# A six-layer Perceiver block on one core: experts' scores asked for one tile further ahead, unit rows on GpSimd, context loads in the scores' loop, two bias products moved forward

## The reference, cut to what matters

```python
x = x + L0_xattn(layernorm(x), ctx_1024, ...)
x = x + L0_attn(layernorm(x), ...)            # state space
x = x + L0_ffn(layernorm(x), ...)             # soft mixture of 16 experts, 16 slots each
x = x + L1_xattn(layernorm(x), ctx_1024, mask, ...)
x = x + L1_attn(layernorm(x), ...)            # causal attention
x = x + L1_ffn(layernorm(x), ...)             # routed linear, 8 experts

def L0_ffn(x, ln_gamma, ln_beta, mu, scale, w1, b1, w2, b2):
    xn = layernorm(x, ln_gamma, ln_beta)
    x_unit, mu_unit = l2norm(xn, axis=-1), l2norm(mu, axis=0)
    logits = einsum('bnd,des->bnes', x_unit * scale, mu_unit)
    dispatch = softmax(logits, axis=1)                       # over the 32 tokens of a batch
    combine = softmax(logits.reshape(B, N, E * S), axis=-1)  # over the 256 slots
    slot_in = einsum('bnd,bnes->besd', xn, dispatch)
    h = gelu(einsum('besd,edh->besh', slot_in, w1) + b1)
    slot_out = einsum('besh,ehd->besd', h, w2) + b2
    return einsum('besd,bnes->bnd', slot_out, combine)

def L1_ffn(x, tile_sigs, W, b):
    idx = argmax(einsum('bsd,td->bst', x, sign(tile_sigs)), axis=-1)
    return (einsum('bsd,tde->bste', x, W) + b)[.., idx, :]
```

## Time and profile before

| | us |
|---|---|
| median of three runs | 985.24 |
| the three runs | 984.61, 985.24, 1930.26 |
| the profiled execution | 986.62 |
| its span, first to last instruction | 984.8 |

### The profile page before, as it was taken

The page is one execution under the profiler, slowest core; times in us unless marked ns, Lnnn a source line. Parts: engine busy times, 40 slices in busy tenths (PEclk is TensorE's granted clock), DMA queues, the critical chain, the costliest instruction groups (busy, mean ns, idle before and its releaser), DMA issues. The chain is left out here.

```text
span 984.8 us, 25493 instructions
## 1 busy us (share of the span) xinstructions
PE 815.8 (83%) x9286; PEld 448.7 (46%) x9286; DVE 726.6 (74%) x2428; ACT 563.4 (57%) x1419; POOL 201.6 (20%) x216
## 2 busy tenths in 40 slices
PE   5899999998867687887764577789698799999887
PEld 2577777776323233333231255456466334343343
DVE  5688888886389999989999588256565376767856
ACT  3798889889666658458415167445243533333345
POOL 1376676666000000000000012000310000000036
PEclk9999999999978789789867799799699899999989
DMA  8111111100000000000000250400183000000001
GB/s 251 34 40 46 37 43 37 38 21 2 1 0 0 1 0 1 1 1 1 0 1 1 82 99 1 173 4 4 44 322 150 1 1 1 1 1 1 1 13 32
DMA packets 23422, 36.67 MB, mean 37 GB/s; under 512 B 5668, under 2 KB 19748, under 8 KB 21156
## 3 DMA queue, kind: packets, MB, share of 16 engines
q1 hardware_dynamic: 23336, 35.53, 11.7%
HBM read 34.48 MB, written 1.05 MB: 36 GB/s over the span
## 5 line engine op out<-in xcount | busy, mean ns | idle before, releaser
L496 ACT ACTIVATE xa_prob<-xa_s,xa_nmax 128x257 f32<-128x257 f32 x256 | 128.1, 503 | 21.0 <-DVE xa_nmax L633 19.3
L780 POOL TENSOR_TENSOR xa_prob<-xa_prob,xa_rinv 128x1028 f32<-128x1028 f32 x64 | 121.6, 1902 | 76.8 <-DVE xa_rinv L640 75.9
L633 DVE CUSTOM_DVE_ANT_0 xa_s<-xa_s_ps,xa_nbias 128x257 f32<-128x257 f32 x256 | 93.1, 420 | 12.4 <-ACT xa_prob L496 6.4
L1764 POOL TENSOR_TENSOR mo_disp_t<-mo_disp_t,mo_rst 128x256 f32<-128x256 f32 x16 | 9.9, 617 | 362.8 <-DVE mo_rst L1734 362.8
L326 PE MATMUL xa_t_ps<-identity,xa_prob 128*128 128x128 f32 x512 | 69.5, 279 | 3.6 <-ACT xa_p_t L505 1.8
L623 DVE COPY xa_kvs<-xa_kv_ps 128x512 f32<-128x512 f32 x64 | 44.1, 689 | 34.4 <-PE xa_kv_ps L300 34.4
L2523 ACT COPY ca_z<-ca_z_ps 128x512 f32<-128x512 f32 x64 | 37.5, 586 | 50.7 <-PE ca_z_ps L2399 50.7
L326 PEld LDWEIGHTS xa_t_ps<-identity,xa_prob 128*128 128x128 f32 x512 | 54.8, 141 | 25.2 <-issue 25.2
L2399 PE MATMUL ca_z_ps<-ca_xn_t,ca_m_t 128*128 128x512 f32 x128 | 64.2, 631 | 0.7 <-ACT ca_xn_t L2516 0.7
L505 ACT COPY xa_p_t<-xa_t_ps 128x1024 f32<-128x1024 f32 x64 | 63.5, 992 | 1.8 <-PE xa_t_ps L326 1.8
L939 PE MATMUL ss_bank<-ss_xs,ss_wx 128*128 128x512 f32 x128 | 60.2, 620 | 5.0 <-DVE ss_eps L1393 3.1
(11 more groups left out here) (369 smaller groups left out, 1898.6 us busy)
## 6 DMA issues: line engine op xcount, KB each, us to landing
xa_ctx_t<-in_ctx_t SPq DMA_DIRECT2D x64, 128.5 KB, 2.1
room<-in_ctx_t SPq DMA_DIRECT2D x8, 1028.0 KB, 6.5
room<-in_ctx_n SPq DMA_DIRECT2D x8, 1024.0 KB, 4.7
ss_wx<-in_ss_wx SPq DMA_DIRECT2D x1, 2048.0 KB, 7.7
xres<-in_x SPq DMA_DIRECT2D x4, 256.0 KB, 5.3
out_x<-xres SPq DMA_DIRECT2D x4, 256.0 KB, 2.3
ma_mask_u<-in_mask SPq DMA_DIRECT2D x4, 128.5 KB
room<-in_ca_wk SPq DMA_DIRECT2D x1, 512.0 KB, 3.5
```

The source lines that it names most:

```text
L496: nc.scalar.activation(prob[:, r, g, :], s_sb[:, b, g, :], ACT.Exp, bias=nmax[:, r, g:g + 1], scale=-1.0, accum_out=rsum[:, r, g:g + 1]).t ...
L633: nc.vector.tensor_tensor_reduce(out=s_sb[:, b, g, :], in0=s_ps[:, g, 0:S], in1=nbias[:, g, :], scale=1.0, scalar=3e38, op0=ALU.add, op1=A ...
L780: nc.gpsimd.tensor_tensor(prob[:, r, :, :], prob[:, r, :, :], bc(rinv[:, r, :].rearrange("p (g o) -> p g o", o=1), (P, G, S)), ALU.mult).t ...
```

## The change

Four edits, none of which adds or takes away arithmetic.

1. Scores one tile further ahead. PE transposes the unit rows of tile t+3 (not t+2) in turn t and computes the scores of tile t+2 ahead of the transposes of tile t's results. Three tiles are transposed before the loop instead of two. ACT copies tile t+3's transposed rows, takes the exponentials of tile t+1, and only then the squares (turn 5) or the roots (now turn 6).
2. Twelve of the thirteen unit rows of ACT go to POOL (one multiplication per tile, in the turn before its own), the other to DVE, ahead of the loop. On DVE what rides along (centring, scaling, the two tiny steps) now stands between `maxima` and `scales` of a turn instead of behind them. The scores' two PSUM buffers are banks 0 and 2 of `mo_lj_ps`, not 0 and 1, and the joins use neighbouring banks.
3. The four context loads are issued by SP in the first block, as soon as the eighth join's products are done, not in the second block.
4. In the routed layer the bias products of tiles 0 and 1 come ahead of the experts' products of the same tile.

```diff
-            return lj_ps[:, n % 2:3:2 - n % 2, SLOTS:2 * SLOTS].rearrange("p s (i c) -> p s i c", i=2)
+            return lj_ps[:, n % 2:n % 2 + 2, SLOTS:2 * SLOTS].rearrange("p s (i c) -> p s i c", i=2)
...
-        l_ps = lj_ps[:, 0:2, :]
+        l_ps = lj_ps[:, 0:3:2, :]
...
+        @block.sync
+        def _(sp):
+            sp.wait_ge(join_mm, JOINS)
+            for keys_first in (False, True):
+                for u in range(2):
+                    load_context(sp, d, ctx, u, u, keys_first)
...
-                    last = nc.tensor.matmul(lj_ps[:, 2 if h % 2 else n % 2, SLOTS + h // 2 * D:SLOTS + h // 2 * D + D],
+                    last = nc.tensor.matmul(lj_ps[:, n % 2 + h % 2, SLOTS + h // 2 * D:SLOTS + h // 2 * D + D],
...
-            for t in range(2):
-                turn_x(t, t)
-                logits(t, t)
+            turn_x(0, 0)
+            turn_x(1, 1)
+            logits(0, 0)
+            turn_x(2, 0)
+            logits(1, 1)
 
             for t in range(T):
-                if t + 2 < T:
-                    turn_x(t + 2, t % 2)
-                turn(t, t % 2)
+                if t + 3 < T:
+                    turn_x(t + 3, 1 - t % 2)
                 if t + 2 < T:
                     logits(t + 2, t % 2)
+                turn(t, t % 2)
                 if FIRST <= t < FIRST + JOINS:
                     join(t - FIRST)
...
             xut(0, 0)
             xut(1, 1)
+            xut(2, 0)
             exps(0, 0)
 
             for t in range(T):
+                if t + 3 < T:
+                    xut(t + 3, 1 - t % 2)
+                if t + 1 < T:
+                    exps(t + 1, 1 - t % 2)
                 if t == 5:
                     last_squares()
-                if t == 7:
+                if t == 6:
                     last_roots()
-                if t + 2 < T:
-                    xut(t + 2, t % 2)
-                if t + 1 < T:
-                    exps(t + 1, 1 - t % 2)
-                if t + 3 < T:
-                    unit(t + 3, 1 - t % 2)
                 out(t, t % 2)
...
             unit(2, 0)
+            unit(3, 1)
             maxima(0, 0)
             scales(0, 0)
 
             for t in range(T):
                 if t + 1 < T:
                     maxima(t + 1, 1 - t % 2)
-                if t + 1 < T:
-                    scales(t + 1, 1 - t % 2)
-                if FIRST <= t < FIRST + JOINS and t % 2 == 1:
-                    joined_values(t - FIRST)
                 if t < 2:
                     centred(AHEAD + 2 * t)
                     centred(AHEAD + 2 * t + 1)
...
                 if t == 7:
                     last_units()
+                if t + 1 < T:
+                    scales(t + 1, 1 - t % 2)
+                if FIRST <= t < FIRST + JOINS and t % 2 == 1:
+                    joined_values(t - FIRST)
 
         @block.gpsimd
         def _(pool):
+            def unit(t, j):
+                pool.wait_ge(xut_mm, t - 1)
+                if t == AHEAD:
+                    pool.wait_ge(unit_ready, 1)
+                nc.gpsimd.tensor_scalar(xu[:, j, :], x1[:, t, :], sums[:, t:t + 1], None, ALU.mult).then_inc(xu_ready, 1)
+
             for t in range(T):
+                if 0 < t and t + 3 < T:
+                    unit(t + 3, 1 - t % 2)
                 pool.wait_ge(rst_ready, t + 1)
...
             for t in range(T):
+                if t < 2:
+                    own_bias(t)
                 experts(t)
-                own_bias(t)
+                if t >= 2:
+                    own_bias(t)
```

19 lines of the change are left out of this document (4 added, 15 removed).

## The result

The changed kernel takes 975.94 us (median of 4 runs, 974.84 to 976.36) against 985.11 us of the kernel before: a ratio of 0.989 over all runs, with a 95% interval from 0.9872 to 0.9908. By the medians that is 9.2 us less, twice the 4.5 us of the forecast. It lies between the two prices of the rival in which PE's gaps in the second block go with the loads (977.0 us for half of them, 973.4 us for all), and by the 2% bound it counts as no change.

A forecast was written before the change was run, and what follows sets the result against it. DVE was taken to bound the scores' block and PE the second block. Savings of 2.16 + 1.76 - 0.25 + 0.86 = 4.53 us from 985.24 gave 980.7 us (chance 0.66), with a range from 975.0 to 984.6 us.

The forecast's parts named there:

- PE's gaps in the second block go with the loads: Rival, second block: PE's 7.3 us of gaps vanish with the context loads, 973.4 us, half of it 977.0; chance 0.14.
- Context loads: Scores' block: SP issues the loads some 11 us sooner, nothing waits for them either way; counted as nothing.
- Riders between maxima and scales: Scores' tiles 1 to 4 on DVE: 3.63 to 3.09 us each, four save 2.16 us (0.88 at the other end).
- Squares behind the exponentials: Scores' tile 6: 3.45 us in place of 5.21, 1.76 us saved, of which 0.6 might be lost.
- Unit rows on POOL: Scores' loop: ACT loses 13 multiplications, POOL gains 12; no gain or loss for unit rows from 0.29 up to 2 us.
- Scores one tile ahead: Scores' block: gains nothing by itself, costs 0.25 us once at the start, between 0.1 and 0.4.
- Library reload: POOL reloads its library in front of the first unit row; counted as nothing, after a gap of 0.27 us before.
- POOL starts late: Rival, scores' loop: a reload of two turns (5.58 us) gives back 3.2 us of the gain, 983.9 us; chance 0.08.
- Bias products first: Routed layer: DVE starts on tile 2 sooner, PE's wait of 0.86 us goes; 0.86 us saved, between 0.2 and 1.0.
- Slower: the gaps spread: Rival, second block: the nine calm tiles get PE's gaps too, 11.0 us more, 991.7 us; chance 0.05.
- the change doesn't do what it says: Rival: riders hide nothing, squares still hold DVE, only the bias products help, 984.4 us; chance 0.07.

## Why the prediction was right and wrong, point by point

- *Context loads*: the step that failed. The prediction put the move of the loads at nothing; the second block gave 8.0 us (7.6 us in the profile of the kernel with this edit alone, 8.3 us by its median). "I count nothing" left out that a fetch of PE's program that comes late beside the loads sets PE back for several tiles. The rival had it at 7.3 us and a chance of 0.14. Both of its observations against were true, and neither was against it: the gaps go on with a DMA share of 0.02 because the lag outlives the loads, and they fall at fixed distances because PE's program is fetched in pieces of fixed length. I took "it comes at fixed places" for "it is not caused by something in time". A fetch that is late once stays late in each piece until a place in the list that gives it back, and both signs follow from that.
- *Riders between maxima and scales*: right in kind, 2.9 us in place of 2.16. A tile became 2.90 and not 3.09 us. I added two durations of 0.30 us, but in a row of such instructions the next starts before the one ahead of it has ended by its row: from 567.72 to 568.31 us two that show 0.67 us together push the reciprocal back by 0.59, and in later tiles by 0.52. The pair also hid in 0.30 us of wait plus the end of the subtraction.
- *Squares behind the exponentials*: 1.90 us for tile 6, forecast 1.76. But it isn't theirs alone. With the slack of the other two edits the squares cost 0.58 us ahead of the exponentials. The gain of 1.9 is what the moves give together.
- *Unit rows on POOL*: counted 0, worth 0.71 us in the loop, since ACT's lateness had cost 0.15 us at each join and 0.3 at tile 8. The length was 0.61 and not 0.3 us. "Up to 2 us alike" fell: at 1.8 us the loop lost 1.77 us, through DVE's instructions and not through a wait.
- *Scores one tile ahead*: 0.27 us at the start as forecast (0.25). Together with the unit rows it was not without gain.
- *Library reload*: right, a gap of 0.07 us. *POOL starts late* did not come.
- *Bias products first*: 0.94 us in the layer, forecast 0.86, but that is luck. The layer before had 6.0 us of low clock and after 2.9 us; against the kernel with the loads alone and 3.0 us of it the gain is 39.43 - 39.30 = 0.13 us. PE's wait did not go; it grew from 0.86 to 1.47 us, because PE was done sooner and DVE's reading moved with it. And 1.7 us were lost between the second block and the layer. The edit has no visible part in that: the changed kernel with the bias products put back took 251.50 us there, near the 251.83 of after, and the same code took from 250.15 to 255.02 us over all profiles of this study. By the whole time the edit is not measurable.
- *Slower: the gaps spread* did not come; nor did *the change doesn't do what it says*.
- Without the loads' term the sum was close: 4.9 to 5.3 us measured for the rest, 4.5 forecast. That is in part luck. The loop, the start and the layer gave 5.29 - 0.27 + 0.94 = 5.96 us by the stages, 1.4 more than forecast, and stages that the change leaves alone lost 3.3 us in this execution. The range held the time, since it reached into the rival.

## What to carry to other kernels

Where PE runs hundreds of short products in a few microseconds, read its unexplained gaps together with the packets of its instruction queue, and keep bulk loads away from the moment of a fetch. The price is not paid during the load alone but, in the first half of the block here, in every piece behind it. Issue such loads beside a stage whose engines run few and long instructions, as the scores here, whose tiles stayed at 2.79 us with 4 MB in flight. And before a wait of PE is counted as time to be won, compare the granted clock with and without it.

## What the runs showed of the hardware that I had not expected

- A fetch of PE's program (by the reading of the packets above) that fell into 1 to 4 MB of loads some microseconds old came late, by some 2 to 3.5 us, and PE stood still until 0.9 to 1.6 us behind its end. Where it did so in the first half of the block, the pieces behind it had gaps of 0.3 to 1.6 us, up to the eighth piece, and the fifteen tiles lost 4.1 to 8.0 us; in the second half they lost 3.7 us and no lag stayed. Three kernels (squares back, unit rows on ACT, three multiplications on POOL) had two or three such gaps, 0.9 to 2.0 us in all, with no load in the block at all, and the same packets late by some 140 to 155 instructions; their fifteen tiles took 58.57, 58.88 and 56.82 us. A fourth (riders back) had one of 0.48 us. The largest of these gaps:

```profile
637.47 0.98 PE L1849 MATMUL me_so_ps<-me_slot_out,mo_comb_t 128*64 128x128 f32 x13 [1.00 <-issue]
```

  So loads are one way to a late fetch and not the only one. What made it late in those four stays open.
- GpSimd beside DVE: DVE's TENSOR_SCALAR of 256 columns, which reads one tensor, went from 410 to 449 ns in the median and to 560 at worst, when POOL was busy with 1.2 us more per turn. The Trainium skill ("GPSIMD Engine Reference", section 1 "Specifications") names contention with DVE's instructions that read two tensors from SBUF or run in a mode with two ports; this one reads a single tensor, and no run here shows its mode.
- GpSimd's multiplication of 128 columns by a column took 0.60 to 0.61 us, where its copy of as many took 292 ns.
